# A recurrent attention block on one core: two ternary products moved in TensorE's written order, and the steps of hidden chunk 2 moved on ScalarE and VectorE

## The reference

```python
xn = layernorm(x)
q, k, v = split(xn @ Wqkv + bqkv)
qp, kp = elu(q) + 1, elu(k) + 1
kv  = kp^T v          (per sequence)      k_sum = sum of kp over the sequence
attn = (qp @ kv) / (qp . k_sum + 1e-6)
z = layernorm(xn + attn) * g1 + b1
ffn = (silu(z @ Wg + bg) * (z @ Wu + bu)) @ Wd + bd
s = layernorm(z + ffn) * g2 + b2
w = ternary(W) * mean|W|                   (ternary: -1, 0 or 1)
out = x + s * silu(xn @ w^T)
```

## Time and profile before

| | us |
|---|---|
| median of 3 runs (1208.1 to 1210.26) | 1210.11 |
| the profiled execution | 1209.84 |
| its span | 1208.1 |
| TensorE busy | 1187.2 (98%) |
| VectorE busy | 1079.5 (89%) |
| ScalarE busy | 953.2 (79%) |
| GpSimd busy | 843.7 (70%) |

### The profile page before, as it was taken

One profiled execution on the slowest core, in us unless ns is written; L12 is line 12 of the kernel. 1 busy time (PEld: TensorE's weight loads), 2 busy tenths in 40 slices (PEclk: granted clock), 3 DMA queues, 4 the chain that ended last, 5 costly groups with the idle time before them and its releaser, 6 DMA issues.

```text
span 1208.1 us, 24021 instructions
## 1 busy us (share of the span) xinstructions
PE 1187.2 (98%) x7550; PEld 1067.3 (88%) x7550; DVE 1079.5 (89%) x2467; ACT 953.2 (79%) x1557; POOL 843.7 (70%) x994
## 2 busy tenths in 40 slices
PE   8999999999999999999999999999999999999997
PEld 6889998989988999988989989899988999888886
DVE  6988999999999999999999999999999999777765
ACT  7787888878888888888878888788887878867753
POOL 3443787767787776787757887677886767766676
PEclk9999999999999999999999999999999999999999
DMA  7213432334432334432334432244332343222201
GB/s 216 78 48 88 123 106 70 88 106 123 123 104 72 88 106 123 122 105 73 88 106 122 110 103 83 75 123 123 109 96 67 97 123 105 71 71 63 76 21 36
DMA packets 137523, 115.61 MB, mean 96 GB/s; under 512 B 12339, under 2 KB 122293, under 8 KB 137398
## 3 DMA queue, kind: packets, MB, share of 16 engines
q1 hardware_dynamic: 137398, 114.08, 32.6%
HBM read 67.38 MB, written 46.67 MB: 94 GB/s over the span
## 4 chain that ended last, share of the span: by engine, by line
PE 52%; DVE 21%; ACT 11%; issue 9%; DMA 3%; POOL 2%; SPq 1%; DVEq 0%; ACTq 0%; POOLq 0%
PE bank L1271 36%; PE d_bank L1271 11%; PE xk_bank L1271 5%; DVE st L922 3%; DVE bank L1095 3%; ACT rz L695 3%; DVE rz L1054 2%; DVE h_l L1105 2%; DMA xa<-z_turned 2%; DMA z_turned<-xa 2%; ACT h_h L695 1%; DVE zT_l L1085 1%; ACT ku L695 1%; POOL norm L569 1%; ACT hs L695 1%
## 5 line engine op out<-in xcount | busy, mean ns | idle before, releaser
L1271 PE MATMUL bank<-zT_h,wgu_h 128*128 128x512 f32 x704 | 275.1, 391 | 1.1 <-DVE rz L1054 1.1
L1271 PE MATMUL bank<-zT_l,wgu_h 128*128 128x512 f32 x704 | 275.1, 391 | 0.0
L1271 PE MATMUL bank<-zT_h,wgu_l 128*128 128x512 f32 x704 | 275.0, 391 | 0.0
L695 ACT ACTIVATE rz<-rz,norm 128x256 f32<-128x256 f32 x252 | 140.5, 595 | 53.6 <-DVE norm L1131 53.6
L569 POOL TENSOR_TENSOR norm<-ve,consts 128x4 f32<-128x4 f32 x64 | 72.9, 1139 | 154.7 <-DVE ve L933 154.5
L1271 PE MATMUL d_bank<-wd_h,h_h 128*128 128x256 f32 x640 | 179.4, 280 | 0.1
L1271 PE MATMUL d_bank<-wd_h,h_l 128*128 128x256 f32 x640 | 179.2, 280 | 0.0
L1271 PE MATMUL d_bank<-wd_l,h_h 128*128 128x256 f32 x640 | 179.2, 280 | 0.0
L1095 DVE SCALAR_TENSOR_TENSOR bank<-bank,hb,hs 128x512 f32<-128x512 f32 x160 | 117.9, 754 | 53.6 <-ACT hs L695 41.9
L695 ACT ACTIVATE h_h<-bank 128x512 fp32r<-128x512 f32 x160 | 95.7, 598 | 80.7 <-DVE bank L1095 80.4
L1271 PEld LDWEIGHTS bank<-zT_l,wgu_h 128*128 128x128 f32 x704 | 132.2, 188 | 28.1
(11 more groups left out here) (163 smaller groups left out, 3571.8 us busy)
## 6 DMA issues: line engine op xcount, KB each, us to landing
xq<-in_L_attn_x_dram SPq DMA_DIRECT2D x32, 512.0 KB, 5.9
xa<-in_L_attn_x_dram SPq DMA_DIRECT2D x31, 512.0 KB, 3.9
out_dram<-rz SPq DMA_DIRECT2D x31, 512.0 KB, 5.0
z_turned<-xa SPq DMA_DIRECT2D x120, 128.0 KB, 3.3
xa<-z_turned SPq DMA_DIRECT2D x30, 512.0 KB, 4.1
turned<-xa SPq DMA_DIRECT2D x108, 128.0 KB, 2.4
xa<-turned SPq DMA_DIRECT2D x27, 512.0 KB, 3.9
rz<-in_L_attn_Wg_dram SPq DMA_DIRECT2D x1, 640.0 KB, 5.7
```

The lines of the kernel that those rows point to most:

```text
L695: return eng.activation(out_, in_, func, **kw).then_inc(S[name], 1)
L1271: ins = eng.matmul(dst, left, right, start=first and n == 0, stop=last and n == len(pairs) - 1, **kw)
```

## The change

In TensorE's list B 0 (ternary 0) moves from between G 2 and U 2 to between Q 1 and G 3, where B 1 was; B 1 moves to between XK 1 and XK 2. On ScalarE silu_tern 0 moves from between h_high 1 and last_rows 2 to between q_high 0 and q_high 1, where silu_tern 1 was; silu_tern 1 moves to between h_high 3 and x_high 1; h_high 2 moves ahead of q_exp 0. On VectorE h_low 2 moves ahead of k_max 1. The lists of the first and the last iteration, GpSimd's and SyncE's lists stay. No instruction is added or removed.

```diff
 TENSOR_JOBS = steps("""
-    K 0, D 4, KV 0, KV 1, D 5, K 1, N 0, N 1, N 2, N 3, G 0, U 0, G 1, U 1, G 2, B 0, U 2, Q 0, Q 1,
-    B 1, G 3, D 0, D 1, U 3, G 4, XK 0, U 4, XK 1, XK 2, XK 3, GU 5, D 2, TZ 0, TZ 1, D 3""")
+    K 0, D 4, KV 0, KV 1, D 5, K 1, N 0, N 1, N 2, N 3, G 0, U 0, G 1, U 1, G 2, U 2, Q 0, Q 1,
+    B 0, G 3, D 0, D 1, U 3, G 4, XK 0, U 4, XK 1, B 1, XK 2, XK 3, GU 5, D 2, TZ 0, TZ 1, D 3""")
 SCALAR_STEPS = steps("""
     xk_copy 0, zT_high 0, zT_high 1, x_res 0, x_res 1, kv_high 0, kv_high 1, x_res 2, x_res 3, k_exp 0,
-    last_rows 0, silu_gate 0, h_high 0, silu_gate 1, last_rows 1, h_high 1, silu_tern 0, last_rows 2,
-    silu_gate 2, last_rows 3, k_exp 1, k_high 0, q_exp 0, h_high 2, z_rows 0, z_rows 1, z_rows 2,
-    z_rows 3, q_exp 1, k_high 1, q_high 0, silu_tern 1, q_high 1, silu_gate 3, silu_gate 4, x_high 0,
-    h_high 3, x_high 1, h_high 4, silu_gate 5, xn_high 0, xn_high 1, h_high 5""")
+    last_rows 0, silu_gate 0, h_high 0, silu_gate 1, last_rows 1, h_high 1, last_rows 2, silu_gate 2,
+    last_rows 3, k_exp 1, k_high 0, h_high 2, q_exp 0, z_rows 0, z_rows 1, z_rows 2, z_rows 3, q_exp 1,
+    k_high 1, q_high 0, silu_tern 0, q_high 1, silu_gate 3, silu_gate 4, x_high 0, h_high 3, silu_tern
+    1, x_high 1, h_high 4, silu_gate 5, xn_high 0, xn_high 1, h_high 5""")
 VECTOR_STEPS = steps("""
 ...
-    k_max 1, h_low 2, k_low 0, q_elu 0, z_turn 0, q_elu 1, q_low 0, k_low 1, h_rows 3, h_rows 4,
-    q_low 1, h_low 3, x_low 0, h_rows 5, x_low 1, h_low 4, h_low 5""")
+    h_low 2, k_max 1, k_low 0, q_elu 0, z_turn 0, q_elu 1, q_low 0, k_low 1, h_rows 3, h_rows 4, q_low
+    1, h_low 3, x_low 0, h_rows 5, x_low 1, h_low 4, h_low 5""")
```

## The result

Four runs of the changed kernel took 1219.51 to 1221.47 us, median 1220.87; on the same chip the kernel before took 1209.11 (1208.06 to 1210.26, four runs). The ratio is 1.0097, 95% interval 1.0085 to 1.011. The forecast was 1221.6. The profiled execution took 1221.47 with a span of 1219.7, 11.6 us more than the 1208.1 before.

The account below looks back on a forecast made before the run. TensorE's load and a loop through VectorE's q_elu 0, G 4 and GU 5 bound the kernel. 25 iterations x 0.59 = 14.8 us, less 3 recovered, gives 11.8 more: 1221.6 us, range 1213 to 1228.

Parts of the forecast that it names:

- The loop over G 4: GU 5's end through VectorE's list to q_elu 0, G 4 and next GU 5: period 35.68 grows by 0.59 to 36.27.
- VectorE's gain of 0.19: Ahead of q_elu 0, last_offset 2 and k_max 1 trade at the port; q_elu 0 ends at 567.26, 0.19 us earlier.
- 25 iterations: Middle stretch of 906 us with VectorE's slices at 9: 25 iterations pay 0.59 each, 14.8 us; none before or behind.
- The recoveries: Old delays from a late VectorE come back as time saved: between 0 and 4.9 us, taken as 3.
- The waits of zT_low: zT_low waited 4.9 us in 7 cases; its transfers get 0.8 us more, above the mean case, below the longest.
- The second reason given: VectorE late between q_elu 0 and h_rows 5 no longer counts, having about 1 us to wait there; within the 3.
- ScalarE's tail: Rival C: x_high 0 to silu_gate 5, lengthened by silu_tern 1, makes silu_gate 5 0.2 to 0.3 late; 1228, chance 0.09.
- The order at the port: At VectorE and GpSimd's shared port, last_gate 2 goes before k_low 0, which stays long; rival B, reversed order: 1210.5, chance 0.08.
- the chunk 2 moves: h_high 2 ahead of q_exp 0, h_low 2 ahead of k_max 1: h_low 2 covers U 3's wait, VectorE gains 0.19.
- the 0.3 us of margin: G 4 starts at 567.77, 0.32 us after q_elu 0 frees its bank at 567.45; tightest shown is 0.25.
- Ternary 1 inside the loop: Ternary 1 now lies between G 4 and GU 5 on TensorE, adding 0.94 us where neither ternary job was.
- Ternary 0's move: Ternary 0 leaves its place between G 2 and U 2; U 2 to Q 1 move 0.94 us ahead, at no cost.

Follow-up runs that it names:

- the gate wait: The changed kernel, with GpSimd's last_gate 2 made to wait until k_low 0 has finished: 1208.79 us, ratio 1.0.
- the shortest kernel: The changed kernel with q_elu 0 ahead of k_low 0 on VectorE and GpSimd's last_gate 2 waiting for k_low 0: 1205.71 us, ratio 0.9982.
- the last kernel: The kernel before with q_elu 0 ahead of k_low 0 on VectorE and GpSimd's last_gate 2 waiting for k_low 0: 1216.12 us, ratio 1.0058.
- the chunk-2-only kernel: The kernel before with only h_high 2 ahead of q_exp 0 and h_low 2 ahead of k_max 1: 1219.63 us, ratio 1.0088.

## Why the prediction was right, step by step

- **The loop over G 4.** The signs that it named are there: G 4 0.06 behind q_elu 0, a first matmul of 0.50, a gap of 0.57, no wait of Q 1, a pause of 0.83 ahead of h_rows 5. Its terms: GU 5's end to q_elu 0's end 28.04 us (28.10 reckoned: 28.29 less 0.19), G 4's start to GU 5's end 8.18 (8.12 reckoned: 7.07, 0.94 and the longer matmul), hand-over 0.06 (0.05). The sum is 36.28 against 36.27.
- **VectorE's gain of 0.19** was 0.25. The trade at the port came out as reckoned, k_max 1 at 0.70 and k_low 0 at 1.23; the rest is that last_offset 2 started 0.06 us earlier. That the real sum hung on this is shown by the gate wait: with k_low 0 at 0.68 nothing of the loss was left.
- **25 iterations.** 24 waits of 14.2 us in total. Iteration 22 is the exception: VectorE was delayed less by GpSimd there (its second zT_low took 0.68 for 1.18), and the period is 35.68. From GU 5's end in iteration 0 to that in iteration 25 the time grew by 12.2 us (11.8 reckoned). The filling up to iteration 0 added 0.4 and iterations 26 to 31 gave back 1.0; I had counted both at 0, and they nearly cancel.
- **The recoveries**, taken as 3, were 2.8 (25 x 0.60 less 12.2), but not mainly where the prediction looked first. The waits of zT_low fell from 4.9 to 1.9 us, yet 1.8 of that was in iterations 28 and 29, outside the 25, and what went away within them was worth 0.1 in iterations 9 and 10 and 0.4 in iteration 22 (36.06 before). The second reason given, a VectorE late between q_elu 0 and h_rows 5, brought 1.8, in iterations 5, 15 and 25: in the kernel before, h_rows 5 came 0.5 to 0.7 late in iterations 4, 14 and 24, with a q_low 1 of 1.27 and 1.30 in the last two, and of 1.07 behind a late h_rows 3 in the first. The last 0.6 is the missing wait of iteration 22. So the sum was right in part by luck.
- **ScalarE's tail** just does not bind, as worked out: silu_gate 5 starts at 582.27, and both h_high 4 ahead of it and GU 5 are done at 582.24. With silu_tern 1 out of the tail the time stayed at 1219.9.
- **The order at the port.** k_low 0 pays (1.23) behind a last_gate 2 that was queued before it, and last_offset 2 no longer pays (0.74), as the prediction had it. The Trainium skill, "SBUF — State Buffer", section "Who interferes with whom", puts it as "Issue order, not op shape, decides who blocks." By that rule, the trace agrees where the order can be read: sum_k 2 takes 1.19 when it starts 0.13 us behind q_low 1. Where q_low 1 takes 1.28 the two starts are the same to 0.01 us, and no run shows which was issued first.
- **What it did not see.** It called the chunk 2 moves a gain of 0.19 and nothing else. Alone they cost 10.5 us, over the second loop, through silu_gate 3 and h_rows 3. That loop was the tighter of the two in the kernel before: it had no room at 35.68 (nor had TensorE, whose own jobs take 35.65), while the loop over G 4 had the 0.3 us of margin that the prediction read. In the changed kernel the second loop is short again: its first part is 578.56 - (582.99 - 36.28) = 31.85 in place of 32.41, and with q_low 1 at 1.07 it comes to some 35.5, below 36.28. The reason is on ScalarE, which now does one silu_tern between h_high 1 and silu_gate 3 in place of two: these two start 13.64 us apart, and 557.39 to 571.60 was 14.21.

```profile
564.14 0.60 ACT L695 ACTIVATE h_h<-bank 128x512 fp32r<-128x512 f32 x1 [0.41 <-DVE bank L1095]
...
577.78 1.26 ACT L695 ACTIVATE hs<-bank,hb 128x512 f32<-128x512 f32 x2
```

No sentence of the prediction had that cover, and here it was lucky. Without the cover the number would have come out much the same, though that is argued and not shown: the second loop alone asks for 36.26, the first for 36.28.
- **Ternary 1 inside the loop** was the right place but told too simply. Ternary 0's move was put down at no cost; with it left undone the kernel takes 1207.84, with ternary 1 still between G 4 and GU 5. The move of ternary 0 changes no load, but by the ring it decides which bank G 4 gets. The cost needs both: the late bank and the longer way behind it.

## What to carry to other kernels

Where two engines are full, look for every closed loop that is as long as the period, not for the first one: the time follows the longest, so costs of single edits neither add up nor survive a change of the others. Before a job is moved in a ring, write down the new neighbour of every job, and ask how much work stands behind the one with the latest neighbour. When VectorE and GpSimd both read SBUF, 0.14 us of shift can decide which one pays 0.5 us; a wait that fixes the order on the engine with room took 12 us off one kernel here and put 8 us on another, so look what the delayed instruction meets next.

## What the runs showed of the hardware beyond that

The 256-column matmuls of D and K came closer together in some kernels. Two rows of D 2 in the kernel before, ten matmuls apart, and two of the changed kernel, nine apart:

```profile
539.36 0.28 PE L1271 MATMUL d_bank<-wd_h,h_h 128*128 128x256 f32 x1
...
540.54 0.28 PE L1271 MATMUL d_bank<-wd_h,h_l 128*128 128x256 f32 x1
```

```profile
546.72 0.28 PE L1271 MATMUL d_bank<-wd_l,h_h 128*128 128x256 f32 x1
...
547.74 0.28 PE L1271 MATMUL d_bank<-wd_l,h_h 128*128 128x256 f32 x1
```

That is 0.118 and 0.113 us a matmul. The stretches of 7.74 us from about GU 5's end on, as windows (busy us and count of TensorE, weight loads, VectorE, ScalarE and GpSimd; granted clock; DMA share; GB/s), before and after:

```profile
539.06:546.80 7.74, 7.74 (x68) 7.74 (x67) 7.61 (x11) 5.73 (x12) 4.65 (x5) 1.00 0.57 197
```

```profile
545.96:553.70 7.74, 7.74 (x70) 7.74 (x70) 6.89 (x9) 6.48 (x13) 4.38 (x4) 1.00 0.52 178
```

The granted clock is 1.00 in both, so it is not the clock. Over D 2 to K 1 it is some 0.25 us an iteration. Counted in the D jobs right behind GU 5, in iterations 0 to 24, the quick form stood in 24 of 25 iterations of the changed kernel, in 25 where ternary 1 was moved alone and nothing waited, in 11 of the shortest kernel, and in none of the kernel before. In my expectation for the last kernel I tied it to a pause of TensorE; the kernel with ternary 1 alone speaks against that. Another tie holds through all fourteen kernels: it stood there, in 11 to 25 iterations, in the eight that have ternary 1 between XK 1 and XK 2, and never in the six that have it elsewhere. (The K jobs further on were quick in some iterations of four of these six as well: 1 of the kernel before, 12 of the chunk-2-only kernel.) In the changed kernel it saves nothing, since the loop over G 4 sets the period. Its cause stays open.
